# Attention kernel on one core: ScalarE writes the f16 high half of all eight key tiles, VectorE casts none

## What is computed

```
x = x + L0(gn(x))   # windowed attention: rows of 32 tokens, 8 heads of 32 channels, then a projection with bias
x = x + L1(gn(x))   # attention of all 1024 tokens of an image to one another:
                    #   q, k = 32 channels each, v = 256 channels
                    #   energy = k q^T; attn = softmax(energy); out = gamma * attn v
```

## Time and profile before

| | us |
|---|---|
| median of 3 executions | 676.5 (675.51 to 678.45) |
| the profiled execution | 673.91 |
| its span in the profile | 672.1 |
| TensorE busy | 590.7 (88%) |
| VectorE busy | 470.2 (70%) |
| ScalarE busy | 349.4 (52%) |
| GpSimd busy | 196.2 (29%) |
| mean granted TensorE clock | 0.957 of full |

### The profile page before, as it was taken

One profiled execution on the slowest core, in us unless ns is written; L12 is line 12 of the kernel. 1 busy time (PEld: TensorE's weight loads), 2 busy tenths in 40 slices (PEclk: granted clock), 3 DMA queues, 4 the chain that ended last, 5 costly groups with the idle time before them and its releaser, 6 DMA issues.

```text
span 672.1 us, 15153 instructions
## 1 busy us (share of the span) xinstructions
PE 590.7 (88%) x5859; PEld 426.5 (63%) x5859; DVE 470.2 (70%) x765; ACT 349.4 (52%) x486; POOL 196.2 (29%) x194
## 2 busy tenths in 40 slices
PE   2797845799999999999999999999999999649987
PEld 2465723457775777668676777577766767427756
DVE  4565378577868787788868796878768875764462
ACT  2662245375358643874278535865287414641462
POOL 7422034103352324420450335231452142001303
PEclk9799867899999999999999999999999999769989
DMA  6113323033223313224223313331322231201101
GB/s 211 38 41 96 95 63 86 20 76 96 55 81 102 103 25 96 76 60 111 62 67 89 94 46 87 93 91 44 96 68 60 53 84 60 51 1 41 48 0 63
DMA packets 40308, 47.53 MB, mean 71 GB/s; under 512 B 6848, under 2 KB 32320, under 8 KB 40256
## 3 DMA queue, kind: packets, MB, share of 16 engines
q1 hardware_dynamic: 35280, 41.37, 23.5%
q10 hardware_dynamic: 4976, 5.44, 2.6%
HBM read 10.09 MB, written 8.39 MB: 27 GB/s over the span
## 4 chain that ended last, share of the span: by engine, by line
PE 66%; DVE 16%; issue 5%; ACT 4%; SPq 4%; DMA 3%; ACTq 1%; POOL 0%; DVEq 0%; POOLq 0%
PE pb L275 10%; PE pb L276 9%; PE pb L277 9%; PE pa L275 6%; PE pa L277 6%; PE pa L276 6%; DVE max_neg L1039 4%; PE pa L541 4%; PE pb L589 3%; PE pa L508 3%; PE pb L607 3%; SPq L335 3%; PE pb L429 2%; PE pa L429 2%; DVE ast L941 2%
## 5 line engine op out<-in xcount | busy, mean ns | idle before, releaser
L275 PE MATMUL pb<-v_h,e_h 128*128 128x257 f16 x464 | 127.5, 275 | 0.0
L277 PE MATMUL pb<-v_h,e_l 128*128 128x257 f16 x464 | 126.5, 273 | 0.0
L276 PE MATMUL pb<-v_l,e_h 128*128 128x257 f16 x464 | 126.1, 272 | 0.0
L1039 DVE TENSOR_REDUCE max_neg<-pb 128x1 f32<-128x1024 f32 x64 | 77.6, 1213 | 56.2 <-PE pb L589 56.0
L1054 DVE TENSOR_TENSOR e_l<-e,e_h 128x1024 f16<-128x1024 f32 x64 | 77.9, 1224 | 19.4 <-ACT e L834 18.0
L843 ACT ACTIVATE qk_h<-pb,y_fac 128x256 f32<-128x256 f32 x58 | 27.5, 474 | 110.0 <-DVE y_fac L1061 109.6
L1251 POOL TENSOR_TENSOR y<-qk_h,y 128x256 f32<-128x256 f32 x64 | 46.4, 728 | 117.7 <-ACT qk_h L843 117.6
L834 ACT ACTIVATE e<-pb,f_energy 128x1024 f32<-128x1024 f32 x64 | 71.3, 1114 | 16.3 <-PE pb L607 16.3
L1232 POOL TENSOR_TENSOR xb<-xin,bias 128x2048 f32<-128x2048 f32 x8 | 36.3, 4533 | 143.4 <-DVE x L1019 142.8
L1237 POOL TENSOR_TENSOR before_turn<-before_turn,a_rinv 128x1024 f32<-128x1024 f32 x16 | 30.6, 1913 | 107.0 <-DVE a_rinv L1000 101.2
L833 ACT ACTIVATE e_h<-pb,f_energy 128x1024 f16<-128x1024 f32 x40 | 44.5, 1114 | 22.9 <-PE pb L607 22.9
(11 more groups left out here) (152 smaller groups left out, 1365.8 us busy)
## 6 DMA issues: line engine op xcount, KB each, us to landing
xin<-in_x SPq DMA_DIRECT2D x15, 512.0 KB, 4.6
diag<-qkT SPq DMA_DIRECT2D x60, 128.0 KB, 2.4
diag<-turned SPq DMA_DIRECT2D x60, 128.0 KB, 2.4
turned<-before_turn SPq DMA_DIRECT2D x120, 64.0 KB, 2.0
out<-y SPq DMA_DIRECT2D x24, 256.0 KB, 2.2
out<-y ACTq DMA_DIRECT2D x8, 256.0 KB, 2.1
q_stack<-qk_hl SPq DMA_DIRECT2D x8, 128.0 KB, 2.3
k_stack<-qk_hl SPq DMA_DIRECT2D x8, 128.0 KB, 2.3
```

Source lines behind the costliest of these rows:

```text
L275: nc.tensor.matmul(out_ap, lh, rh, start=start, stop=False)
L276: nc.tensor.matmul(out_ap, lh, rl, start=False, stop=False)
L277: return nc.tensor.matmul(out_ap, ll, rh, start=False, stop=stop)
L1039: nc.vector.tensor_reduce(max_neg[:, it:it + 1], pb[:, 0:2, :].rearrange("p a n -> p (a n)"), X, ALU.max, negate=True).then_inc(b_max, 1)
```

## The change

`DVE_HIGH` lists the key tiles whose high half VectorE casts. It becomes empty. For tiles 1, 3 and 4 of every image ScalarE now issues the activation of L833 ahead of that of L834, as it did for the other five, and VectorE's cast of L1052 is not issued. The semaphores `b_exp` and `b_el` are raised by the same instructions as before; `b_eh` is no longer used.

```diff
@@ -43,7 +43,7 @@
 HEADS, DH = 8, 32
 WIN = 32
 GROUP = 8
-DVE_HIGH = (1, 3, 4)
+DVE_HIGH = ()
 VCOL = CH + 2
 EPS = 1e-5
 ROW_SCALE = 2.0 ** 15
```

## The result

The changed kernel takes 695.45 us (median of 4 executions, 691.32 to 697.95) against 676.0 us for the kernel before (4 executions): a ratio of 1.0277, 95% interval 1.0215 to 1.034. It is slower by 19.5 us; the forecast was 695 us. A second series further down gives 1.0295. The ratios here leave out executions in a slower state (one of "tile 1 only" took 1028.84 us, at a mean granted clock of 0.563) that the medians beside them take in, so a ratio can differ by up to 0.4% from the quotient of the two medians.

A forecast was written before the change was run, and what follows sets the result against it. TensorE bounds the kernel, with ScalarE just in time to release its PSUM banks. Terms 13.5 + 1.3 + 2.5 + 1.4 = 18.7 us on 676.5 give 695.2, say 695; own range 690 to 700, 8 in 10 within 687.5 to 700.5.

The forecast's parts named there:

- Removed casts, taken as 0: 24 casts on VectorE, 16.5 us in all: no gain, since TensorE doesn't wait for them; bound 2.0 us a step.
- Tile 1, a stall of 1.01: Steady image: tile 1's new activation delays the bank release, so tile 2's energies come 1.01 us late.
- Tile 4, covered: Steady image: 1.29 us of slack before tile 5's energies, while TensorE projects, takes tile 4's added activation; no stall.
- Tile 6, a stall of 0.7: Steady image: ScalarE ends tile 5 +2.7 to +2.8 us late, so tile 6's energies stall TensorE another 0.7.
- Steady images, 5 x 2.7 = 13.5: Images 1 to 5: the stalls before the energies of tiles 2, 4 and 6 cost 2.7 us an image, 13.5 together.
- Image 0, +1.3: Tile 5's energies come 2.8 us late, but the projection's DMA wait of 1.52 takes 1.5 back.
- Image 6, +2.5: TensorE already waits for ScalarE between tiles 2 and 5: three activations count 3.0 us, less 0.54 of DMA wait.
- Image 7, +1.4: Tile 1's activation adds 1.0 us, tile 3's is covered by output matmuls, tile 4's adds 0.4.
- rival B: Clock falls in the steady images: 7.5 us on top of the forecast, 702 us; chance 0.07.
- Rival A: Waits on VectorE, 2.0 us a step, shrink in the steady images and give delay back: 685 us; chance 0.09.
- C: Faster: VectorE is the real hold-up, its waits shrink by at most 2.0 us a step, to 660 us; chance 0.03.
- D: No change: effects cancel or matmuls behind make up TensorE's late energies, 676.5 us; chance 0.02.

The follow-up runs named there:

- A second series: The changed kernel run once more with more rounds, against the kernel before: 694.24 against 673.89 us, ratio 1.0295.
- tile 1 only: Against the kernel before, only tile 1's high half goes to ScalarE, VectorE still casts tiles 3 and 4: 681.72 us, ratio 1.0085.
- last image on VectorE: Kernel before, but in the last image VectorE casts the high halves of all eight tiles: 673.45 us, ratio 0.9993.
- no cast: Kernel before, with VectorE's casts of tiles 1, 3, 4 made for image 0 alone and not replaced: 676.57 us, ratio 0.9994.
- cast kept: Changed kernel, with VectorE still making dummy casts for tiles 1, 3, 4; against the kernel before: 692.45 us, ratio 1.0254.
- all on VectorE: Kernel before, but VectorE casts the high halves of all eight tiles in every image: 678.03 us, ratio 1.0054.

## Why the prediction was right

By its own steps:

- *Removed casts, taken as 0:* right; the removal alone gave 0.9994 and the dummy casts cost nothing in the steady steps (75.75 against 75.72).
- *Tile 1, a stall of 1.01:* the wait is 0.91 and the delay 2.81 - 1.80 = 1.01 (364.99 to 367.80, against 352.72 to 354.52 in the kernel before).
- *Tile 3, another 1.01:* a wait of 1.05; tile 4's energies come 2.95 after tile 3's (370.83 to 373.78), 1.01 more than in the kernel before (359.50 - 357.56 = 1.94).
- *Tile 4, covered:* right, 3.05 between the energies of tiles 4 and 5 as before.
- *Tile 6, a stall of 0.7:* the term that was too large; it measured 3.42 - 3.06 = 0.36 (376.83 to 380.25 against 362.55 to 365.61), and another 0.09 came ahead of tile 7. I took ScalarE's backlog as given back by the 0.20 idle ahead of v_h only. The next instruction in its timeline before, which I had not counted, hid another wait inside a merged pair:

```profile
361.95 1.49 ACT L788 ACTIVATE qkT<-pa,f_q 128x512 f32<-128x512 f32 x2
```

  The pair takes 1.49 us there, and 1.27 for the pair ahead of it and for the same pair in the changed kernel: 0.22 us of idle time, which I read as the second copy's wait for TensorE. From the +3.03 of tile 4, both gaps leave +2.6 at tile 5 in place of the forecast's 2.7 to 2.8. Measured from tile 0's energies, ScalarE was +2.4 there (379.04 - 361.94 = 17.10, against 364.34 - 349.67 = 14.67 in the kernel before), so another 0.2 came back in small pieces along its row of instructions.
- *Steady images, 5 x 2.7 = 13.5:* measured 4 x 2.42 + 2.47 = 12.2; this is the mis-sized term of tile 6, five times.
- *Image 0, +1.3:* 75.45 - 73.89 = 1.56. The DMA wait of 1.52 is gone: the projection follows tile 5's energies at once (149.83, then 150.27).

```profile
149.83 0.60 PE L607 MATMUL pb<-k_stack,q_stack 98*128 98x512 f16 x2 [0.91 <-ACT e L834]
150.27 0.27 PE L275 MATMUL pa<-wp_h,turned 128*128 128x256 f16 x1
```

- *Image 6, +2.5:* 2.77, and 2.51 in the second profile. In the first, the energies of tiles 2, 4 and 5 come 1.01, 1.01 and 1.44 later after the ones ahead of them, 3.46 and not 3.0, and the interval behind them is 0.67 shorter. The 0.44 too much lies where tile 4's energies ran at the lower clock (1.03 us long, against 0.61), so that this total came out near the forecast is in part luck.
- *Image 7, +1.4:* 1.06 and 0.94. Tile 1's 1.01 and tile 4's 0.40 are there; tile 3's was more than covered, the interval behind it is 0.38 shorter.
- *The sum, 18.7:* from the first energies to the end 560.4 - 542.9 = 17.5, and 17.3 in the second. The medians differ by 19.5 and 20.4. That the median hit the forecast to half a microsecond is luck: the steps alone would give 694, and the 2 to 3 us between are not explained by the steps of these profiles. One possible source, not shown, is the single profile of the kernel before: "last image on VectorE", the same program up to image 6, has steps 0 and 6 shorter by 1.39 and 1.21.
- *The profiled execution, 692.6:* it took 697.0; the sum has no term for the start. In both profiles of the changed kernel image 0 begins 5.6 to 6.3 us later than in the profile of the one before. Among all the kernels, whose instructions up to there are the same, that start falls near 129 (128.0 to 130.5) or near 134 (133.4 to 135.5), with and without the added activations: "no cast" has none of them and starts at 134.45, "cast kept" has all of them and starts at 128.39. The ten executions of the changed kernel lie in two groups, 691.2 to 693.9 and 696.2 to 698.0, five each. My estimate from a start at 129.2, steps of 560.3 and 1.8 us around the span is 691.3 for an early start, so I take the late one as scatter that the changed kernel shows in half of its executions.
- *The clock in steady images, 1.00:* right. Busy time by stretch, image 3, beside the earlier trace rows:

```profile
362.00:437.00 75.00, 70.69 (x729) 51.66 (x729) 55.25 (x90) 45.31 (x63) 22.90 (x23) 1.00 0.28 75
```

The signs were ScalarE busy about 376 and VectorE 454; they are 372.1 and 455.6. The first took 1.11 us for an activation, where 1.01 from start to start is what it adds. (The 702 of rival B is 695.2 + 7.5 = 702.7.)

Rival A (given back later) falls with steps of 75.7; B (the clock) with this row; C and D with the direction, and C also with "no cast". The rule in the Trainium skill, "Perfetto Trace Analysis", Identifying the Most-Contended Engine, that the engine of highest occupancy is the one to improve, doesn't help here. By busy matmuls TensorE leads at 88%, and it is what waits; the page holds that figure to be a poor measure of TensorE's headroom and goes by the matmul work done against the peak, not worked out here, and by the weight loads, 63% here, by which VectorE leads at 70%. ScalarE, last by either count at 52%, was the one without reserve.

## What to carry to other kernels

Before moving work to an idler engine, look up on its timeline who is waiting at the end of each instruction that will be later, and how many tenths of a microsecond that waiter had in reserve: in this kernel the price of an instruction was the time it added (1.01 us) less that reserve, hand-over by hand-over, and not a matter of occupancy. Where one engine frees a shared buffer and then has more to do with its contents, freeing the buffer first may help, but look up how the rest travels as a backlog: here it took 10.3 us off the sum of steps and only 0.6 of 2.4 us off a steady one. In counting a backlog's way back, look inside merged rows of a timeline: a pair that lasts longer than its like can hide a wait.

## What I had not expected of the hardware

The same instructions on the same engines took 1.6 us longer in one execution than in another through the clock. The last image of "all on VectorE" and of "last image on VectorE" are the same program, and TensorE's idle stretch ahead of tile 3's energies is the same (busy 0.63 and 0.62 us in the third stretch); in the six stretches of 2 us ahead of it, at 1.00 in both, it is busy for 11.92 us in each. Busy time by stretch of 2 us from tile 0's energies on, with TensorE's granted clock as the third value from the end. All on VectorE:

```profile
644.80:646.80 2.00, 0.63 (x4) 0.11 (x2) 1.86 (x3) 1.57 (x3) 0.56 (x1) 1.00 0.00 0
646.80:648.80 2.00, 0.91 (x9) 0.61 (x8) 1.97 (x4) 1.11 (x1) 0.00 (x0) 1.00 0.00 0
648.80:650.80 2.00, 2.00 (x19) 1.58 (x17) 1.97 (x3) 0.06 (x1) 0.00 (x0) 1.00 0.00 0
```

Last image on VectorE:

```profile
634.70:636.70 2.00, 0.62 (x4) 0.11 (x2) 1.81 (x3) 1.61 (x3) 0.29 (x1) 1.00 0.00 0
636.70:638.70 2.00, 0.91 (x7) 0.54 (x6) 1.97 (x4) 1.12 (x1) 0.00 (x0) 0.93 0.00 0
638.70:640.70 2.00, 2.00 (x11) 1.42 (x10) 1.97 (x3) 0.00 (x0) 0.00 (x0) 0.50 0.00 0
```

In the second the clock is at its lower level (1.2 GHz) for the matmuls behind the idle stretch, 11 of them in 2 us in place of 19; in the first it stayed at 2.4 GHz. That makes tile 4's energies come 5.25 us after tile 3's in place of 3.69, and the last step 36.48 in place of 34.83. So after much the same idle time the clock fell in one execution and stayed in the other. The same is seen ahead of image 0, where all kernels have the same instructions. The kernel before and the changed kernel, busy time in 120 to 128:

```profile
120.00:128.00 8.00, 4.86 (x110) 2.98 (x98) 4.59 (x6) 1.94 (x2) 0.00 (x0) 1.00 0.01 2
...
120.00:128.00 8.00, 6.59 (x95) 4.19 (x91) 3.49 (x3) 0.00 (x0) 1.27 (x3) 0.50 0.01 2
```

The five profiles with a late start (133.4 to 135.5) all have 0.50 in this stretch, the seven with an early one 0.89 to 1.00. The changed kernel's profile is 1.84 us late at one of the energies for the row maxima (118.80 against 116.96) and 5.56 us at tile 0's transposed energies (134.76 against 129.20), so most of the lateness arises around this stretch. What tips the clock one way or the other was not found.

So steps 0, 6 and 7 scatter by 1 to 2 us between executions and the work ahead of image 0 by up to 7.5, while the steady steps, always at 1.00, repeat to 0.1 us in their mean (73.30, 73.22 and 73.24 in the three kernels whose images 1 to 4 cost TensorE the same). A change that works in every step is read better from those steps than from a median of four.
